# Apply stage: products multiplied two at a time, a step of one and a step of the next in turn, into two PSUM banks

## The reference: what is computed

```python
base  = einsum('bsi,oi->bso', x, weight) + bias                 # cond
low   = einsum('bsi,bri->bsr', x, lora_a[adapter_id])           # rank 16
h     = base + scale[:, None, None] * einsum('bsr,bor->bso', low, lora_b[adapter_id])
w     = (NF4[codes].reshape(-1, 64) * absmax[:, None]).reshape(2048, 2048)
out   = x + einsum('bsd,od->bso', h, w) + bias2
```

## Time and profile before

| what | value |
|---|---|
| median of 3 runs | 2221.19 us (2220.89 to 2225.11) |
| profiled execution | 2220.52 us |
| its span, first to last instruction | 2218.7 us |
| mean granted TensorE clock | 0.993 of full |
| PE / DVE / ACT busy | 98% / 81% / 46% of the span |
| matmuls, weight loads | 12104 each |
| DMA | 558 MB, 251 GB/s mean |

### The profile page before, as it was taken

How to read it: one execution, slowest core, us unless ns; L and a number is a source line. 1 busy time by engine, 2 the same in 40 slices (tenths; PEclk the granted TensorE clock), 3 DMA queues, 4 the chain that set the end, 5 groups by cost and what they waited for, 6 DMA issues and landing times.

```text
span 2218.7 us, 31547 instructions
## 1 busy us (share of the span) xinstructions
PE 2168.3 (98%) x12104; PEld 1861.6 (84%) x12104; DVE 1790.6 (81%) x2655; ACT 1016.1 (46%) x1277; POOL 36.7 (2%) x47
## 2 busy tenths in 40 slices
PE   4899999999999999999999999999999999999999
PEld 3688778787878787899999988888988889888888
DVE  8899879768975574688787888888898887888887
ACT  7655555555553333444444434343443334433332
POOL 3100000000000000000000000000000000000000
PEclk8899999999999999999999999999999999999999
DMA  9678788887887897877777887777987778877775
GB/s 262 223 241 260 244 253 259 266 258 241 261 264 239 282 299 228 268 246 230 243 238 238 268 279 241 243 251 242 293 258 248 245 246 256 293 248 246 240 243 173
DMA packets 381172, 558.00 MB, mean 251 GB/s; under 512 B 23376, under 2 KB 234992, under 8 KB 380896
## 3 DMA queue, kind: packets, MB, share of 16 engines
q1 hardware_dynamic: 377712, 544.95, 77.6%
q0 software_dynamic: 3312, 11.03, 1.6%
HBM read 427.96 MB, written 128.99 MB: 251 GB/s over the span
## 4 chain that ended last, share of the span: by engine, by line
PE 92%; DMA 3%; DVE 2%; ACT 1%; issue 1%; SPq 1%; ACTq 0%; DVEq 0%
PE ps L1417 26%; PE ps L1249 14%; PE ps L1251 14%; PE ps L1250 14%; PE ps L1418 13%; PE ps L1421 4%; PE ps L1264 2%; PE ps L1420 2%; PE ps L1297 1%; DMA rq<-xc_d 1%; PE ps L1245 1%; ACT wq_nat_w L673 1%; DMA xr<-xc_d 0%; DMA code_w<-in_L_ffn_codes_dram 0%; DMA xc_d<-rq 0%
## 5 line engine op out<-in xcount | busy, mean ns | idle before, releaser
L1417 PE MATMUL ps<-comb,xs 128*128 128x512 f32 x2527 | 903.3, 395 | 0.8 <-DVE comb L1015 0.8
L734 ACT CAST xs<-xr 128x1024 fp32r<-128x1024 f32 x427 | 448.4, 1051 | 623.3 <-DMA xr<-xc_d 622.5
L1418 PE MATMUL ps<-comb,xs 128*128 128x256 f32 x2527 | 707.8, 280 | 0.0
L1021 DVE TENSOR_TENSOR xs<-xr,xs 128x1024 fp32r<-128x1024 f32 x427 | 521.4, 1222 | 125.8 <-ACT xs L734 123.1
L1417 PEld LDWEIGHTS ps<-comb,xs 128*128 128x128 f32 x2527 | 474.3, 188 | 103.5 <-DVE comb L1015 1.1
L1418 PEld LDWEIGHTS ps<-comb,xs 128*128 128x128 f32 x2527 | 475.4, 188 | 14.5
L1249 PE MATMUL ps<-wq,tile 128*128 128x512 f32 x1088 | 467.9, 430 | 4.7 <-DVE tile L955 4.0
L1251 PE MATMUL ps<-wq,tile 128*128 128x512 f32 x1088 | 427.2, 393 | 0.0
L1250 PE MATMUL ps<-wq,tile 128*128 128x512 f32 x1088 | 426.1, 392 | 0.0
L1249 PEld LDWEIGHTS ps<-wq,tile 128*128 128x128 f32 x1088 | 205.3, 189 | 73.1 <-issue 7.0
L1251 PEld LDWEIGHTS ps<-wq,tile 128*128 128x128 f32 x1088 | 204.9, 188 | 45.0
(11 more groups left out here) (119 smaller groups left out, 2212.5 us busy)
## 6 DMA issues: line engine op xcount, KB each, us to landing
xr<-xc_d SPq DMA_DIRECT2D x427, 512.0 KB, 3.9
raw<-in_L_cond_weight_dram SPq DMA_DIRECT2D x128, 512.0 KB, 4.7
xc_d<-rq SPq DMA_DIRECT2D x26, 1792.0 KB, 7.5
res<-in_x_dram SPq DMA_DIRECT2D x64, 512.0 KB, 5.3
out_dram<-res SPq DMA_DIRECT2D x128, 256.0 KB, 4.5
wc_d<-cs SPq DMA_DIRECT2D x32, 896.0 KB, 4.7
comb_raw<-wc_d SPq DMA_DIRECT2D x28, 1024.0 KB, 8.0
x_nat<-in_x_dram SPq DMA_DIRECT2D x104, 256.0 KB, 3.9
```

Of the source, the lines that this page charges most:

```text
L734: nc.scalar.copy(xs[f][:, HI, :, :], xr[f][:, LO, :, :]).then_inc(s_xhi, 1)
L1021: tt(xs[f][:, LO, :, :], xr[f][:, LO, :, :], xs[f][:, HI, :, :].bitcast(F32), ALU.subtract).then_inc(s_xlo, 1)
L1417: nc.tensor.matmul(bank[:, :], x_hi, both, start=(k == 0), stop=False)
L1418: nc.tensor.matmul(bank[:, 0:HW], x_lo, high, start=False, stop=False)
```

## The change

Before, the eight steps of product f were followed by the eight steps of product f + 1. Now the products of a tile pair are taken as (0, 1), (2, 3), (4, 5) and (6). The waits of both products of a group come first, then step k of the one and step k of the other in turn. What followed f = 3, 5, 1 and 6 on TensorE (transpositions, low-rank multiplications) follows the group in which it is. The matmuls themselves, the banks, and the orders on the other four queues stay as they were.

```diff
-            for i in range(PRODUCTS):
...
-                if i >= 5:
-                    pe.wait_ge(s_ev, i - 4)
-                pe.wait_ge(s_xlo, split_of(i) + 1)
-                if is_wide(i):
-                    for k in range(HK):
...
+            def wait_product(i):
+                pp, f = divmod(i, NF)
+                j, p = divmod(pp, PAIRS)
                 if p == 0:
                     pe.wait_ge(s_clo, NF * j + f + 1)
                 if j == 0 and p % 2 == 0 and f in WITH_LOW:
...
                 if i >= 5:
                     pe.wait_ge(s_ev, i - 4)
                 pe.wait_ge(s_xlo, split_of(i) + 1)
-                if is_wide(i):
+
+            def multiply_product(i, k):
+                f = i % NF
+                bank = bank_p[i % 5]
+                room, cols = columns(i)
+                x_hi, x_lo, high = xs[f][:, HI, k, :], xs[f][:, LO, k, :], cw[f][:, k, HI, cols]
+                if not is_wide(i):
+                    last = three(bank[:, room], x_hi, x_lo, high, cw[f][:, k, LO, cols], k == 0, k == HK - 1)
+                elif k < HK - 1:
+                    nc.tensor.matmul(bank[:, :], x_hi, cw[f][:, k, :, cols], start=(k == 0), stop=False)
+                    last = nc.tensor.matmul(bank[:, 0:HW], x_lo, high, start=False, stop=False)
+                else:
+                    nc.tensor.matmul(bank[:, 0:HW], x_lo, high, start=False, stop=False)
+                    last = nc.tensor.matmul(bank[:, :], x_hi, cw[f][:, k, :, cols], start=False, stop=True)
+                if k == HK - 1:
+                    last.then_inc(s_prod, 1)
+
+            for pp in range(ALL_PAIRS):
+                for fs in ((0, 1), (2, 3), (4, 5), (6,)):
+                    for f in fs:
+                        wait_product(NF * pp + f)
                     for k in range(HK):
...
+                        for f in fs:
+                            multiply_product(NF * pp + f, k)
+                    if pp < PAIRS and 3 in fs:
+                        transpose_low(2 * pp)
+                    if pp < PAIRS and 6 in fs:
+                        transpose_low(2 * pp + 1)
+                    for f in fs:
+                        if lora_after(NF * pp + f) is not None:
+                            multiply_lora(lora_after(NF * pp + f))
```

More of the change, by code:

```diff
@@ L1394, in _, with columns @@
             pe.wait_ge(s_evac, evacs(JOBS - 1))
-            for i in range(PRODUCTS):
+            def columns(i):
                 pp, f = divmod(i, NF)
                 j, p = divmod(pp, PAIRS)
-                bank = bank_p[i % 5]
                 if j == 0 and f in WITH_LOW:
[L1400 to L1404, removed]
+                    return slice(0, EXT), slice(0, EXT) if p // 2 % 2 == 0 else slice(R, COLS)
+                return slice(0, HW), slice(R, R + HW) if f in WITH_LOW else slice(0, HW)
+            def wait_product(i):
+                pp, f = divmod(i, NF)
+                j, p = divmod(pp, PAIRS)
                 if p == 0:
```

## The result

The changed kernel takes 2237.41 us (median of 4 runs, 2234.91 to 2239.68), the kernel before 2221.24 us. The ratio is 1.0068, with a 95% interval of 1.0056 to 1.0080: 15 to 16 us slower. 2228.6 us was predicted, with a range of 2221.5 to 2241.

What follows compares the result with a forecast made beforehand. TensorE, busy 98% of the span, was taken to bound the kernel. Losses of 2.7 + 2.8 + 2.3 + 0.3 = 8.1 us on the profiled 2220.5 us gave 2228.6 us, range 2221.5 to 2241.

Steps and rivals of the forecast that it cites:

- Rival 3: Apply stage: a matmul going to another bank starts 5 ns sooner, 2688 changes return 13.4 us, giving 2215 us; chance 0.06.
- the start: Start of the apply stage: a group needs its second product's weights up to 2.82 us earlier; 0.3 us lost.
- (a): Each group: the odd product (f = 1, 3, 5) has its waits one product earlier, by 2.82 us.
- (b): Each group: the even product ends 2.47 us later, delaying the load into its slot and its addition on VectorE.
- rival 2: Strip 0: VectorE 0.8 us late in each of 15 inner tile pairs, adding 12 us, giving 2240 us; chance 0.15.
- strip 1: Change from strip 0: 1.7 us at the low-rank multiplication plus 0.6 at group (4, 5), 2.3 us lost.
- strip 2: Change from strip 1: 2.0 us lost at group (4, 5), 2.7 us in all with VectorE's lateness one tile pair later.
- strip 3: Change from strip 2: 2.15 us lost at f = 4 plus 0.7 from VectorE's lateness, 2.8 us in all.
- the shift of f = 5's weights: Change to strip 2: f = 5's weights issued 1.1 us later, shifting their cast, split and the addition of f = 0 by 1.1.
- Rival 1: Changes of strip and start: loads land when they do now, the DMA being the limit; 2.5 us lost, 2223.0 us; chance 0.19.
- The clock: Apply stage: granted clock at 1.2 GHz for a tenth of 1311 us, costing about 66 us, giving 2286 us; chance 0.02.
- The backlog of VectorE one tile pair later: After the changes to strips 2 and 3: group (0, 1) waits for the addition of f = 3; about 0.7 us more.

## Why the prediction was right, point by point

**That no time is won by the change of bank** was right. The stretches inside strips 1 to 3 agree to 0.01 us. Rival 3 is out, and so is the reading that the gap of 0.12 us after 256 columns holds a price for the same bank.

**That the loss sits at the changes of strip and at the start** was right, and each of (a) and (b) was shown alone: the waits in pairs cost 7.1 us, late ends 5.1 us (the medians against the kernel before on the same chip, 2222.16 and 2222.49). Together that is 12.2 of 15 to 16 us; the clock fell at strips 2 and 3 only with both. That the middle of a strip costs 0 was right too; rival 2 did not come. Strip 0 even got 0.9 us faster, in p = 3 to 14.

**The sum was too small**, 8.1 against 14.8 us: strip 1 2.3 against 3.3, strip 2 2.7 against 5.5, strip 3 2.8 against 5.4, the start 0.3 against 1.5, less 0.9 in strip 0. The measured 2237.41 us lie above the 2226 to 2234 us that the prediction gave its own case. They are in the range because it was opened to 2241 us for rival 2, which did not come. The places and the kind of the waits were foreseen; that the time falls within the range is in part luck. The step that failed is the shift of f = 5's weights: "about 1571.2 instead of 1570.11: 1.1 us later". It was worked out from SP's queue, as if the load began with its own request. The request came 22.2 - 20.6 = 1.6 us later, the weights 31.2 - 28.4 = 2.8 us. The two kernels with one group alternating show why: the request for f = 0 comes 2.5 us later, the DMA stands nearly idle meanwhile, and it never makes up for that. With 2.8 in the place of 1.1 the prediction's own working gives a wait of 1582.46 + 2.8 - 1581.56 = 3.7 us; the trace has 3.83. Rival 1 had seen that the DMA is loaded, and drew the wrong conclusion, that a later request would not matter: it matters for the first load of the stream and hardly for the fifth.

**The clock** was given 0.02, as a fall for a tenth of the stage. It fell three times for 3.4 us, after waits of 2.7 to 3.8 us, and not through the cycling of banks: it is 1.00 in the kernel that alternates only in inner tile pairs from the start of the stage to the last matmul. Filling the wait with matmuls kept it at 1.00 at strips 2 and 3, which shows idleness as the cause there. The Trainium skill's "TensorE: Matmul & The Clock Gate", section "A second HAM failure mode: psum-queue depth-cycling", is not borne out by this trace as far as the banks go. The three falls took 3 x 1.6 = 4.8 us, but only 2.0 of 3.2 us came back where two of them were avoided.

**The backlog of VectorE one tile pair later**, 0.6 to 0.7 us in the prediction, is not seen in the changed kernel at strips 2 and 3, because the slow clock stands in its place. It shows as soon as either the clock or the late weights are taken away, with 0.3 to 0.6 us a wait.

**The start of the stage**: the wait of 2.73 us came. In return the wait of 0.8 us of the kernel before is gone, as said, and so is one of 1.2 us (L1100). The fall of the clock was not in the term. The prediction read the list of waits as if the 0.8 us stood alone in the apply stage, where the two waits for `low_rep`, 1.2 and 1.0 us, stand beside it. **Strip 1**: `low_st` cost 1.5 us where 1.7 was said, but that is luck as far as the cause goes: the kernel that alternates only in inner tile pairs has 1.6 us there, with no product of the last tile pair ending late. The rest is a wait of 0.8 us at (4, 5), where 0.6 was said, and three gaps of some 0.2 us.

No version beats the kernel before. The alternation in inner tile pairs alone ties with it, and so does, in one execution, the group (4, 5) of the last tile pairs alone.

## What to carry to other kernels

Two accumulations that take turns start and end together: the second's inputs are needed one accumulation early, and what the first frees comes nearly one late. In this kernel it cost nothing to the hundredth of a microsecond where both were covered, so look at the places with the least slack, here where new weights are loaded. There, ask how long the delay leaves the DMA without work, from the first load of the stream on, and not when the load that is waited for is itself issued. And price a wait of some 2 us or more of TensorE with the slow clock behind it.

## What the runs showed of the hardware that was not expected

- After waits of 2.7, 3.8 and 2.9 us of TensorE the granted clock was 0.5 for 3.4 us (1.6 us lost each time). In two experiments it fell after waits of 1.8, 2.0 and 2.2 us as well. It stayed at 1.00 at strip 1's waits of 1.5 and 0.8 us. The length of the wait alone does not decide: with a wait of 1.77 us for `low_st` at the end of strip 0 the clock fell where only the last tile pair alternates, and in the kernel with the filling matmuls, after a wait of the same length at the same place, it did not:

```profile
1246.50:1254.00 7.50, 5.51 (x41) 5.12 (x42) 6.13 (x8) 3.81 (x2) 0.00 (x0) 1.00 1.09 362
```

- Switching the PSUM bank after every one or two matmuls, 504 to 546 more times in 262 us, changed the time by 0.01 us at most in strips 1 to 3. In strip 0, where products of three matmuls of 272 columns alternate with wide ones, twelve tile pairs took 0.9 us less, in all four kernels that alternate there. Why is open.
- In the stream of weights at strip 2 the 16 DMA engines are full (the first window is of the kernel before, the second of the changed one), and delaying the fifth of seven by 2.5 us moved its arrival by 0.1 us, while delaying the first by 2.5 us moved the fifth's by 3.0 and the first four's by 1.1 to 1.3 (one execution each).

```profile
1560.00:1570.00 10.00, 10.00 (x85) 9.96 (x85) 8.34 (x7) 6.20 (x4) 0.00 (x0) 1.00 1.08 351
```

```profile
1566.00:1576.00 10.00, 10.00 (x86) 9.95 (x85) 6.78 (x6) 5.71 (x3) 0.00 (x0) 1.00 1.07 348
```
